# A transformer-like block in fp32r halves: one 64-column stationary for both mLSTM gates, and the last batch's steps in another order

## The chip, the cores and the metric

The kernel runs on one core of one Trainium2 chip. The metric is the device time of one execution in microseconds; several runs are taken and their median is quoted. A profiled execution gives a span, from its first to its last instruction, and a trace of every engine: PE is TensorE, DVE is VectorE, ACT is ScalarE, POOL is GpSimd, SP is SyncE, whose queue issues the DMAs here.

## What is computed

Four layers on 4 batches of 256 tokens, width 256: attention, a gated FFN, an mLSTM block with its own MLP, and an int8 FFN, with a layer norm after each. The change touches the mLSTM block, which in the reference is

```python
h_in = _rmsnorm(x, norm1_w)
q = (h_in @ wq).reshape(B, S, H, dqk).transpose(0, 2, 1, 3)      # k, v alike
o_pre = h_in @ w_og
i_pre = _soft_cap(h_in @ w_ig + b_ig).transpose(0, 2, 1)         # 8 heads, cap * tanh(x / cap)
f_pre = _soft_cap(h_in @ w_fg + b_fg).transpose(0, 2, 1)
h = _mlstm_parallel(q, k, v, i_pre, f_pre)
...
logfg = jax.nn.log_sigmoid(f_pre)
Fcum = jnp.cumsum(logfg, axis=-1)
Dmat = Fcum[..., :, None] - Fcum[..., None, :] + i_pre[..., None, :]     # causal
m = jnp.max(Dmat, axis=-1, keepdims=True)
C = qk * jnp.exp(Dmat - m)
n = jnp.maximum(jnp.abs(jnp.sum(C, axis=-1, keepdims=True)), jnp.exp(-m))
h = jnp.einsum('bhst,bhtd->bhsd', C / n, v)
```

## The kernel before

Every fp32 product is made of three: each operand is held as a high part and a remainder (`xTh`, `xTl`; `WLh`, `WLl`), and PE adds high by high, high by remainder and remainder by high. So `six` issues 6 matmuls for a contraction over 256, and the activations of a batch stand transposed in `xh_v[:, :, c, :]` and `xl_v[:, :, c, :]`, 256 columns for a batch `c`.

Every engine's program is written out by hand in one order, and each engine runs its own in order; semaphores tie them. The stretch that the change touches lies between the end of the first FFN (`ffn_pe(pe, 0)`) and the mLSTM heads:

- **The last batch.** Batches 0 to 2 have been normed and transposed inside the first FFN. Batch 3 comes behind it: `add_out(dve, 0, 3)`, `dve_stats`, `pool_ln`, `dve_apply` (layer norm), `act_ssq`, `pool_rms`, `dve_xs` (rms norm into `xs`), `pe_T(pe, 1, 3)` (4 transposes into the PSUM bank `TB`), `act_hi` and `dve_lo` (the two parts of `xT`, which raise `xt_split`).
- **The projections on PE.** For each batch `project_qk` (2 x 12 matmuls of 256 columns into `UG[0]` and `UG[1]`) and `project_vog` (2 x 6 of 512 columns into `UG[2]` and `UG[3]`). ACT and DVE empty the banks: `evac_q`, `evac_k`, `evac_og` on ACT, `split_q`, `split_k`, `take_v` on DVE. The next batch may write a bank when `qk_split` or `og_ready` says so.
- **The gates.** `project_gates(c)` makes the rows of the input gate and of the forget gate, 8 heads each. A window of a padded weight (`WIDE` = 96 + 128 columns) puts batch `c`'s heads into rows 32c to 32c + 7 of a 128-row sum; both gates and all four batches are added up into two banks, `X[:, 0:S]` and `OUTS[:, 1, 0:S]`: 12 matmuls of 256 columns per batch. When all four are in, ACT's `gates` takes both banks (2 Tanh of 128 x 256), then Exp and Ln, which needs another function table, and loads the table of Tanh again for `evac_og(1)`.
- **The rows.** DVE's `chain` (two scans, two adds) makes the running sums `cumS`, `gr`, their maxima `M` and `nm`. SP writes `M` to DRAM (`scr_m`) and reads it back broadcast over 128 partitions, batch 0 in four quarters (`m_first`), batches 1 to 3 in two halves each (`m_rows`) into the buffer `A[c % 2]`; `m_rows(c, half)` for c > 1 waits on `e_ready`, that is for the decays of batch c - 2 of the same heads. PE's `rows_T` transposes `gr` and `nm`.
- **The MLP's weights.** 12 pieces of 128 x 512 come through a ring of 5 buffers `raw`. ACT takes the high part (`mlp_hi`), POOL the remainder (`split_mlp`), SP loads the next (`more`).
- **The heads.** `heads(c)` runs through 4 pairs of heads. PE: `scores` (L1521, L1522) of the next pair, `values` (L1536 to L1540), `back` of the pair before (L1549), and in between `heads_T` (L1561), `project_out`, `pe_T` of an earlier batch, and a filler `keep_busy` (L1578). ACT: `take_pair`, then `decay` of the two heads that come 4 heads later (L1693, L1694). DVE: `weigh` of two heads (L1880), `mask_rows` (L1871: adds the causal mask to two heads' rows in `A`), and for an earlier batch `norm_b` (L1907, L1912), `hoT`, `head_sums`, `add_heads`. POOL's `head_scales` (L2056) makes the scales that `norm_b` needs, and PE's `heads_T` waits for `norm_b`.

## Time and profile before

| | |
|---|---|
| median of 3 runs | 673.22 us (672.23 to 675.36) |
| the profiled execution | 672.34 us, of which the span is 670.6 us |
| PE busy | 658.1 us, 98% of the span |
| DVE, ACT, POOL busy | 438.3, 411.3, 246.7 us |
| granted TensorE clock, mean | 0.995 |
| last matmuls of the first FFN | 473.42 us |
| projections and gates on PE | 473.76 to 502.92 us |
| heads | 502.92 to 540.70 us |

Times in the trace are microseconds from the start of the span. A matmul's record is longer than the step to the next one, because the array is pipelined and its end is modelled: a 256-column matmul shows 0.28 us, and the next one starts 0.12 us later. What a matmul costs in a full stream is therefore read from start to start.

### The profile page before, as it was taken

How to read it: one execution, taken by the hardware profiler on the slowest of the kernel's cores; microseconds unless marked ns; L12 is line 12 of the kernel's file. 1: busy time of each engine (PE TensorE's matmuls, PEld its weight loads, DVE VectorE, ACT ScalarE, POOL GpSimd, SP SyncE). 2: the span in 40 equal slices, each digit the busy share in tenths (PEclk: the TensorE clock that was granted, in tenths of full speed). 3: DMA queues.
4: the chain of work that ended last, by engine and by line, in shares of the span. 5: the costliest groups of instructions: out<-in, count | busy, mean ns of one | idle time of the engine just before them, and what ended most of it. 6: DMA issues, size and time to landing. Idle time of an engine off the chain costs nothing. (4 is left out here: it accounts for less than half of the span.)

```text
span 670.6 us, 15275 instructions
## 1 busy us (share of the span) xinstructions
PE 658.1 (98%) x5297; PEld 633.0 (94%) x5297; DVE 438.3 (65%) x968; ACT 411.3 (61%) x1085; POOL 246.7 (37%) x279
## 2 busy tenths in 40 slices
PE   8999999999999999999999999999999999999995
PEld 8999999999999999999999899999987799999995
DVE  6556557557666655765665576556569986556877
ACT  5556677666776666866577773334689864333553
POOL 3731972134353133632328555112451462222011
PEclk9999999999999999999999999999999899999999
DMA  7174654435534436534363404000166100000000
GB/s 254 37 219 160 193 172 140 133 101 174 168 127 113 127 108 185 161 128 126 97 183 124 111 1 151 32 0 2 48 208 243 65 1 1 1 1 0 1 33 31
DMA packets 38172, 69.74 MB, mean 104 GB/s; under 512 B 3440, under 2 KB 22640, under 8 KB 37872
## 3 DMA queue, kind: packets, MB, share of 16 engines
q1 hardware_dynamic: 37696, 68.38, 32.8%
q10 hardware_dynamic: 432, 0.79, 0.4%
q8 instruction: 26, 0.43, 0.3%
q14 instruction: 18, 0.15, 0.1%
HBM read 52.18 MB, written 16.97 MB: 103 GB/s over the span
## 5 line engine op out<-in xcount | busy, mean ns | idle before, releaser
L312 PE MATMUL PJ<-xTh,WBh 128*128 128x256 f32 x364 | 106.7, 293 | 0.3 <-POOL WBl L839 0.3
L314 PE MATMUL PJ<-xTh,WBl 128*128 128x256 f32 x364 | 103.0, 283 | 0.0
L313 PE MATMUL PJ<-xTl,WBh 128*128 128x256 f32 x364 | 102.8, 283 | 0.0
L824 POOL TENSOR_TENSOR stage<-stage 128x256 f32<-128x256 f32 x32 | 24.5, 766 | 165.0 <-DVE stage L691 165.0
L584 ACT ACTIVATE probs<-probs,rinv 128x256 f32<-128x256 f32 x128 | 58.4, 507 | 26.7 <-DVE rinv L707 26.7
L1202 PE MATMUL UG<-xTh,WBh 128*128 (+1 forms) x256 | 73.6, 288 | 0.3 <-PEq L54 0.3
L1205 PE MATMUL UG<-xTh,WBl 128*128 (+1 forms) x256 | 72.4, 283 | 0.0
L1203 PE MATMUL UG<-xTl,WBh 128*128 (+1 forms) x256 | 72.4, 283 | 0.0
L1274 ACT ACTIVATE ga<-UG 128x256 f32<-128x256 f32 x64 | 24.5, 383 | 75.1 <-PE UG L1205 75.1
L312 PEld LDWEIGHTS PJ<-xTh,WBh 128*128 128x128 f32 x364 | 69.6, 191 | 0.9 <-issue 0.5
L313 PEld LDWEIGHTS PJ<-xTl,WBh 128*128 128x128 f32 x364 | 69.6, 191 | 0.0
L314 PEld LDWEIGHTS PJ<-xTh,WBl 128*128 128x128 f32 x364 | 69.4, 191 | 0.0
L696 DVE TENSOR_TENSOR QKl<-PJ,QKh 128x512 fp32r<-128x512 f32 x63 | 43.4, 689 | 36.5 <-ACT QKh L572 36.3
L1326 DVE TENSOR_TENSOR gb<-UG,ga 128x256 f32<-128x256 f32 x64 | 27.1, 423 | 44.4 <-ACT ga L1274 43.8
L1061 POOL TENSOR_SCALAR vare<-mv 128x2 f32<-128x2 f32 x13 | 2.9, 224 | 131.9 <-DVE mv L1054 131.9
L839 POOL TENSOR_TENSOR WBl<-raw,WBh 128x512 fp32r<-128x512 f32 x32 | 40.8, 1295 | 28.4 <-ACT WBh L601 28.4
L577 ACT ACTIVATE probs<-TB,nmax 128x256 f32<-128x256 f32 x64 | 29.8, 470 | 33.7 <-DVE nmax L703 32.2
L577 ACT ACTIVATE probs<-SC,nmax 128x256 f32<-128x256 f32 x64 | 29.8, 471 | 32.6 <-DVE nmax L703 32.5
L1202 PEld LDWEIGHTS UG<-xTh,WBh 128*128 128x128 f32 x256 | 49.0, 192 | 0.5 <-issue 0.5
L1203 PEld LDWEIGHTS UG<-xTl,WBh 128*128 128x128 f32 x256 | 49.0, 192 | 0.0
L1205 PEld LDWEIGHTS UG<-xTh,WBl 128*128 128x128 f32 x256 | 49.0, 191 | 0.0
L701 DVE TENSOR_REDUCE rmax<-TB 128x2 f32<-128x512 f32 x32 | 22.1, 692 | 39.8 <-PE TB L393 35.4
(320 smaller groups left out, 2385.9 us busy)
## 6 DMA issues: line engine op xcount, KB each, us to landing
K<-scr_k SPq DMA_DIRECT2D x60, 256.0 KB, 4.3
raw<-in_w_att SPq DMA_DIRECT2D x37, 256.0 KB, 4.7
Q<-scr_q SPq DMA_DIRECT2D x15, 512.0 KB, 7.5
stage<-scr_m SPq DMA_DIRECT2D x6, 768.0 KB, 5.9
scr_q<-rot_h SPq DMA_DIRECT2D x30, 128.0 KB
scr_q<-rot_l SPq DMA_DIRECT2D x30, 128.0 KB
scr_k<-rot_h SPq DMA_DIRECT2D x30, 128.0 KB
scr_k<-rot_l SPq DMA_DIRECT2D x30, 128.0 KB
```

The lines of the kernel that those rows point to most:

```text
L312: pe.matmul(out, ah, bh, start=(i == 0), stop=False)
L313: pe.matmul(out, ah, bl, start=False, stop=False)
L314: last = pe.matmul(out, al, bh, start=False, stop=(i == n - 1))
L577: last = act.activation(probs[:, j % 2, t, :], SC[j % 2][:, t, :], ACT.Exp, scale=SCALE, bias=nmax[:, j % 2, t:t + 1], accum_out=rsum[:, j ...
L584: last = act.activation(probs[:, j % 2, t, :], probs[:, j % 2, t, :], ACT.Copy, scale=rinv[:, j % 2, t:t + 1])
L696: dve.tensor_tensor(part_dst(k, p, False), bank_of(k, p)[:, :], part_dst(k, p, True).bitcast(F32), ALU.subtract).then_inc(part_split, 1)
L824: pool.tensor_tensor(y[:, 0:S], c[:, 0:S], sn[:, S:2 * S], ALU.subtract).then_inc(rope_sum, 1)
L839: pool.tensor_tensor(weights(i, False), raw[:, i % RING, :], weights(i, True).bitcast(F32), ALU.subtract).then_inc(w_split, 1)
L1202: pe.matmul(out, wh, xh_v[:, t, c, :], start=(t == 0), stop=False)
L1203: last = pe.matmul(out, wh, xl_v[:, t, c, :], start=False, stop=(kind == 2 and t == KT - 1))
L1205: last = pe.matmul(out, w_up(kind, t, ht, which, False), xh_v[:, t, c, :], start=False, stop=(t == KT - 1))
L1326: dve.tensor_tensor(y, u, ga[:, ht % 2, 0:S], ALU.mult).then_inc(q["gated"], 1)
```

## The change

Both gates' weights are packed without padding into one stationary of 64 columns (32 for the input gate, 32 for the forget gate; 8 of each are used). One stream through it gives both gates of a batch in 64 rows. `project_gates(0, 2)` takes batches 0 and 1 in one stream of 512 columns, `project_gates(2)` and `project_gates(3)` take 256 each: 6 matmuls a call, 18 in all instead of 48. Each batch has its own region (`gate_sums[c]`: the halves of `X` for batches 0 and 1, the halves of `OUTS[:, 1]` for 2 and 3). ACT's `gates_tanh(c)` copies a batch's 2 x 32 rows through Tanh into rows 32c of `gt`, 8 activations instead of 2. Before `project_gates(3)` writes into the bank of batch 2's sums, PE waits for the Tanh of batch 2.

The rest is order. PE: the gates of batches 0 to 2 stand between the first three parts of the projections, batch 3's in the middle of batch 1's k. ACT: two conversions of MLP pieces move behind batch 0's q and k, the Tanh of batches 0 to 2 stand right behind `act_ssq`, `act_hi(1, 3)` goes ahead of `evac_og(0)`, Exp and Ln stand around `evac_k(1)`, and the conversions of pieces 10 and 11 go into the first two pairs of heads. DVE: `split_q(0)` and `split_k(0)` stand within the last batch's norm. SP: pieces 10 and 11 are loaded behind batch 0's quarters of the rows and ahead of the other batches'. In batch 2's first pair, DVE adds the mask to batch 3's first two quarters ahead of `norm_b(0)`; before, one of them stood behind it and the other one in the next pair.

On PE, where the first projection of batch 0 ended and its v and og parts stood, the kernel before has (`UG<-WLh,xTl` is the end of `project_vog(0)`):

```order
L1457 MATMUL UG<-WLh,xTl 128x512
L1474 MATMUL X<-xTh,WI 128x256
L1474 MATMUL X<-xTl,WI 128x256
L1474 MATMUL X<-xTh,WI 128x256 x2
L1474 MATMUL X<-xTl,WI 128x256
L1474 MATMUL X<-xTh,WI 128x256
L1474 MATMUL OUTS<-xTh,WI 128x256
```

and the changed one (`UG<-xTh,WLl` is the end of batch 0's k, `UG<-WLh,xTh` the start of its v and og):

```order
L1458 MATMUL UG<-xTh,WLl 128x256
L1475 MATMUL X<-xTh,WI 64x512
L1475 MATMUL X<-xTl,WI 64x512
L1475 MATMUL X<-xTh,WI 64x512 x2
L1475 MATMUL X<-xTl,WI 64x512
L1475 MATMUL X<-xTh,WI 64x512
L1456 MATMUL UG<-WLh,xTh 128x512
```

The two sums of 128 rows became one of 64 rows, over two batches at once, and stand ahead of v and og.

On ACT, from the gates to batch 1's og, the kernel before has (`WBh<-raw` is `mlp_hi`, `gt` the gates, `x<-UG` is `evac_og`):

```order
L1736 ACTIVATE WBh<-raw 128x512
L1673 ACTIVATE gt<-X,bgs 128x256
L1673 ACTIVATE gt<-OUTS,bgs 128x256
L1678 ACTIVATE gt<-gt 128x256
L1680 ACT_TABLE_LOAD
L1680 ACTIVATE gt<-gt 128x256
L1667 ACT_TABLE_LOAD
L1667 ACTIVATE x<-UG 128x256 x2
```

and the changed one (`WI<-UG,cols` is `evac_k(1)`):

```order
L1750 ACTIVATE WBh<-raw 128x512
L1684 ACTIVATE gt<-OUTS,bgs 32x256 x2
L1690 ACTIVATE gt<-gt 128x256
L1668 ACTIVATE WI<-UG,cols 128x512
L1694 ACT_TABLE_LOAD
L1694 ACTIVATE gt<-gt 128x256
L1750 ACTIVATE WBh<-raw 128x512
L1675 ACT_TABLE_LOAD
L1675 ACTIVATE x<-UG 128x256 x2
```

Both table loads stay, and between the gates' Exp and Ln stands batch 1's k.

On DVE, in batch 2's first pair, the kernel before has (`stage<-stage,mask` is `mask_rows`, `ho` is `norm_b`):

```order
L1880 SCALAR_TENSOR_TENSOR gb<-UG,ga 128x384 x2
L1907 TENSOR_TENSOR ho<-hraw,hsc 128x256 x2
L1912 SCALAR_TENSOR_TENSOR ho<-x,ho 128x512
L1871 TENSOR_TENSOR stage<-stage,mask 128x2x2x128
L1880 SCALAR_TENSOR_TENSOR rows<-UG,rows 128x384 x2
```

and the changed one:

```order
L1901 SCALAR_TENSOR_TENSOR gb<-UG,ga 128x384 x2
L1892 TENSOR_TENSOR stage<-stage,mask 128x2x2x128 x2
L1928 TENSOR_TENSOR ho<-hraw,hsc 128x256 x2
L1933 SCALAR_TENSOR_TENSOR ho<-x,ho 128x512
L1901 SCALAR_TENSOR_TENSOR rows<-UG,rows 128x384 x2
```

The norm moved behind both masks.

```diff
...
-        gate_w = WI[:, :, :].rearrange("p a n -> p (a n)")[:, 12 * PIECE - 4 * KT * WIDE:]
-        WGh, WGl = (gate_w[:, i * 2 * KT * WIDE:(i + 1) * 2 * KT * WIDE].rearrange("p (t g n) -> p t g n", t=KT, g=2)
-                    for i in range(2))
+        gate_w = WI[:, 11, PIECE - 4 * KT * 32:].rearrange("p (l t n) -> p l t n", l=2, t=KT)
+        WGh, WGl = gate_w[:, 0], gate_w[:, 1]
+        WG_parts = [gate_w[:, l].rearrange("p t (g n) -> p t g n", g=2) for l in range(2)]
...
-        wg_f = stage1[:, 0:2 * KT * WIDE].rearrange("p (t g n) -> p t g n", t=KT, g=2)
+        wg_f = stage1[:, 0:2 * KT * WIDE].rearrange("p (t g n) -> p t g n", t=KT, g=2)[:, :, :, 96:128]
...
-        gate_sums = (X[:, 0:S], OUTS[:, 1, 0:S])
+        gate_sums = [bank[0:2 * 32, i * S:(i + 1) * S] for bank in (X[:, :], OUTS[:, 1, :]) for i in range(2)]
...
-            more(RING, 12)
+            more(RING, 10)
             sp.wait_ge(s_["m_ready"], 1)
             out_rows = scr_m.rearrange("c h n -> (c h) n")
             sp.dma_start(out_rows[:, 0:S], M[:, :]).then_inc(s_["m_out"], 16)
...
             sp.wait_ge(s_["m_out"], 32)
             for quarter in range(4):
                 m_first(quarter)
+            more(10, 12)
             for c in range(1, B):
                 for half in range(2):
                     m_rows(c, half)
...
             def x_parts(c):
                 return [(xh_v[:, t, c, :], xl_v[:, t, c, :]) for t in range(KT)]
-            def project_gates(c):
-
-                pe.wait_ge(s_["xt_split"], N_T[1] + c + 1)
+            def project_gates(c, n=1):
+
+                pe.wait_ge(s_["xt_split"], N_T[1] + c + n)
                 if c == 0:
                     pe.wait_ge(s_["wg_split"], 1)
                     pe.wait_ge(s_["x_added"], N_ADD[3])
-
-                w = slice(96 - 32 * c, 96 - 32 * c + P)
-                for n, out in enumerate(gate_sums):
-                    for i in range(3 * KT):
-                        t, (a, b) = i // 3, ((WGh, xh_v), (WGh, xl_v), (WGl, xh_v))[i % 3]
-                        last = pe.matmul(out, a[:, t, n, w], b[:, t, c, :], start=(c == 0 and i == 0),
-                                         stop=(c == B - 1 and i == 3 * KT - 1))
+                if c == B - 1:
+                    pe.wait_ge(s_["gates_tanh"], B - 1)
+                out = X[0:2 * 32, :] if n == 2 else gate_sums[c]
+                for t in range(KT):
+                    for i, (w, x) in enumerate(((WGh, xh_v), (WGh, xl_v), (WGl, xh_v))):
+                        last = pe.matmul(out, w[:, t, :], x[:, t, c:c + n, :], start=(t == 0 and i == 0),
+                                         stop=(t == KT - 1 and i == 2))
                 last.then_inc(s_["gates_ready"], 1)
-            def project_qk(c):
+            def project_part(c, i, which=range(2)):
                 if c == 0:
                     pe.wait_ge(s_["wl_split"], LP - 1)
-                for i in range(2):
-                    if c:
-                        pe.wait_ge(s_["qk_split"], 2 * c - 1 + i)
-                    for n in range(2):
-                        w = slice((2 * i + n) * P, (2 * i + n + 1) * P)
-                        last = six(UG[i][:, n * S:(n + 1) * S], [(WLh[:, t, w], WLl[:, t, w]) for t in range(KT)],
-                                   x_parts(c))
+                else:
+                    pe.wait_ge(s_["qk_split"], 2 * c - 1 + i)
+                for n in which:
+                    w = slice((2 * i + n) * P, (2 * i + n + 1) * P)
+                    last = six(UG[i][:, n * S:(n + 1) * S], [(WLh[:, t, w], WLl[:, t, w]) for t in range(KT)],
+                               x_parts(c))
+                if which[-1] == 1:
                     last.then_inc(s_["qk_ready"], 1)
...
             def project(c):
-                project_qk(c)
-                project_vog(c)
+                project_part(c, 0)
+                project_part(c, 1)
+                project_vog(c, 0)
+                project_vog(c, 1)
             def rows_T():
...
                     if pair == 1 and c >= 3:
                         pe_T(pe, 2, c - 3)
-            project(0)
-            for c in range(B - 2):
-                project_gates(c)
+            project_part(0, 0)
+            project_part(0, 1)
+            project_gates(0, 2)
+            project_vog(0, 0)
+            project_gates(2)
+            project_vog(0, 1)
             pe_T(pe, 1, B - 1)
-            project_gates(B - 2)
-            project_qk(1)
-            project_gates(B - 1)
-            project_vog(1)
+            project_part(1, 0)
+            project_part(1, 1, range(1))
+            project_gates(3)
+            project_part(1, 1, range(1, 2))
+            project_vog(1, 0)
+            project_vog(1, 1)
             project(2)
             rows_T()
             project(3)
...
         def _(act):
             ffn_act(act, 0)
             act.wait_ge(s_["wg_in"], 16)
-            act.activation(WGh, wg_f, ACT.Copy).then_inc(s_["wg_hi"], 1)
+            act.activation(WG_parts[0], wg_f, ACT.Copy).then_inc(s_["wg_hi"], 1)
             act.wait_ge(s_["small_in"], 16 * 4)
             act.activation(nn[:, 0:1], cols[:, C_LO:C_LO + 1], ACT.Exp)
...
                     act.wait_ge(s_["v_taken"], 2 * c + t + 1)
                     act.activation(og_v[:, c, t, :], UG[2 + t][:, D:2 * D], ACT.Tanh, scale=0.5).then_inc(s_["og_ready"], 1)
-            def gates():
-                act.wait_ge(s_["gates_ready"], B)
-                act.wait_ge(s_["bgs_ready"], 1)
+            def gates_tanh(c):
+
+                act.wait_ge(s_["gates_ready"], max(c, 1))
+                if c == 0:
+                    act.wait_ge(s_["bgs_ready"], 1)
                 for n in range(2):
-                    last = act.activation(gt[:, n, :], gate_sums[n], ACT.Tanh, scale=1.0 / CAP,
-                                          bias=bgs[:, n:n + 1])
+                    at = slice(32 * n, 32 * n + 32)
+                    last = act.activation(gt[32 * c:32 * c + 32, n, :], gate_sums[c][at, :], ACT.Tanh, scale=1.0 / CAP,
+                                          bias=bgs[at, n:n + 1])
                 last.then_inc(s_["gates_tanh"], 1)
-                act.wait_ge(s_["gates_tanh"], 1)
+            def gates_exp():
+                act.wait_ge(s_["gates_tanh"], B)
                 act.activation(gt[:, 1, :], gt[:, 1, :], ACT.Exp, scale=-CAP).then_inc(s_["gates_tanh"], 1)
-                act.wait_ge(s_["gates_tanh"], 2)
+
+            def gates_log():
+                act.wait_ge(s_["gates_tanh"], B + 1)
                 act.activation(gt[:, 1, :], gt[:, 1, :], ACT.Ln, bias=1.0).then_inc(s_["sp_ready"], 1)
             def exp_nm():
...
                         act.wait_ge(ffn_sems[0]["down"], FT * B)
                     act.activation(mlp_place(i, True), raw[:, i % RING, :], ACT.Copy).then_inc(s_["wm_hi"], 1)
-            mlp_hi(0, 5)
+            mlp_hi(0, 2)
+            evac_q(0)
+            mlp_hi(2, 3)
+            evac_k(0)
+            mlp_hi(3, 4)
             act_ssq(act, 1, 3)
-            evac_q(0)
-            evac_k(0)
+            for c in range(3):
+                gates_tanh(c)
+            act_hi(act, 1, 3)
             evac_og(0)
-            act_hi(act, 1, 3)
+            evac_q(1)
+            mlp_hi(4, 5)
+            gates_tanh(3)
+            gates_exp()
+            evac_k(1)
+            gates_log()
             mlp_hi(5, 6)
-            evac_q(1)
+            evac_og(1)
+            evac_q(2)
             mlp_hi(6, 7)
-            evac_k(1)
-            mlp_hi(7, 8)
-            gates()
-            evac_og(1)
-            mlp_hi(8, 9)
-            evac_q(2)
+            evac_k(2)
+            mlp_hi(7, 9)
+            evac_og(2)
             mlp_hi(9, 10)
-            evac_k(2)
-            mlp_hi(10, 12)
-            evac_og(2)
             exp_nm()
             evac_q(3)
             evac_k(3)
...
                     for u in (HM * c + 2 * pair + 4, HM * c + 2 * pair + 5):
                         if u < HM * B:
                             decay(u // HM, u % HM)
+                    if c == 0 and pair < 2:
+                        mlp_hi(10 + pair, 11 + pair)
                     if pair == 2 and c >= 3:
                         act_hi(act, 2, c - 3)
                     if pair == 3 and c >= 2:
...
             dve_stats(dve, 0, B - 2)
             ffn_dve(dve, 0)
             dve.wait_ge(s_["wg_hi"], 1)
-            dve.tensor_tensor(WGl, wg_f, WGh.bitcast(F32), ALU.subtract).then_inc(s_["wg_split"], 1)
+            dve.tensor_tensor(WG_parts[1], wg_f, WG_parts[0].bitcast(F32), ALU.subtract).then_inc(s_["wg_split"], 1)
             dve.wait_ge(s_["small_in"], 64)
             dve.tensor_scalar(bgs[:, :], bg[:, :], 1.0 / CAP, None, ALU.mult).then_inc(s_["bgs_ready"], 1)
...
             add_out(dve, 0, 3)
             dve_stats(dve, 1, 3)
+            split_q(0)
             dve_apply(dve, 1, 3)
+            split_k(0)
             dve_xs(dve, 1, 3)
-            split(0)
+            take_v(0, 0)
+            take_v(0, 1)
             dve_lo(dve, 1, 3)
             split(1)
             chain()
...
                     if c == 0 and pair == 0:
                         mask_rows(0, 2)
                         mask_rows(0, 3)
+                    if (c, pair) == (2, 0):
+                        mask_rows(3, 0)
+                        mask_rows(3, 1)
                     if pair == 0 and c >= 2:
                         norm_b(c - 2)
                     if pair == 1 and c >= 3:
...
                     if c == 0 and pair == 3:
                         mask_rows(1, 2)
                         mask_rows(1, 3)
-                    if c in (1, 2):
-                        mask_rows(c + 1, pair)
+                    if c == 1:
+                        mask_rows(2, pair)
+                    if c == 2 and pair >= 2:
+                        mask_rows(3, pair)
             def finish_heads(k, c, ht):
                 if ht == 0:
```

## Rows read from the trace of the kernel before

**Rows 1.** The page: the span, and the granted clock in 40 slices.
```profile
span 670.6 us, 15275 instructions
PEclk9999999999999999999999999999999899999999
```

**Rows 2.** Stretches: us; busy PE, PEld, DVE, ACT, POOL; clock; DMA share; GB/s.
```profile
503.00:512.00 9.00, 8.79 (x98) 6.78 (x98) 8.46 (x17) 8.57 (x26) 0.00 (x0) 1.00 0.76 297
520.00:524.00 4.00, 4.00 (x29) 2.70 (x27) 3.47 (x7) 2.96 (x9) 0.46 (x1) 0.62 0.61 241
531.00:540.00 9.00, 8.88 (x97) 7.05 (x96) 8.93 (x20) 7.52 (x24) 5.22 (x8) 1.00 0.01 4
560.00:600.00 40.00, 40.00 (x337) 40.00 (x337) 24.12 (x60) 14.81 (x43) 9.48 (x15) 1.00 0.01 2
```

**Rows 3.** Timeline of PE, projections and gates: start, duration, line, operation.
```profile
473.76 0.28 PE L1455 MATMUL UG<-xTh,WLh 128*128 128x256 f32 x1
...
476.63 0.40 PE L1455 MATMUL UG<-WLh,xTh 128*128 128x512 f32 x1
...
479.38 0.29 PE L1474 MATMUL X<-xTh,WI 128*128 128x256 f32 x1
...
482.25 0.60 PE L1119 MATMUL TB<-ident,xs 128*128 128x128 f32 x4
...
486.98 0.28 PE L1474 MATMUL X<-xTh,WI 128*128 128x256 f32 x1
...
488.42 0.40 PE L1455 MATMUL UG<-WLh,xTh 128*128 128x512 f32 x1
...
494.03 0.40 PE L1455 MATMUL UG<-WLh,xTh 128*128 128x512 f32 x1
...
502.92 0.39 PE L1521 MATMUL UG<-WI 32*128 32x256 f32 x2
```

**Rows 4.** Timeline of PE in the heads: stationaries of 33 columns.
```profile
509.40 0.39 PE L1538 MATMUL UG<-gb,V 128*33 128x128 f32 x4
509.62 0.39 PE L1540 MATMUL UG<-gb,V 128*33 128x128 f32 x4
```

**Rows 5.** Timeline of ACT: MLP pieces, the gates' tables, the heads.
```profile
474.57 2.70 ACT L1736 ACTIVATE WBh<-raw 128x512 fp32r<-128x512 f32 x5
...
489.92 1.28 ACT L1680 ACT_TABLE_LOAD   x1
491.22 0.42 ACT L1680 ACTIVATE gt<-gt 128x256 f32<-128x256 f32 x1
...
492.95 0.66 ACT L1667 ACTIVATE x<-UG 128x256 f32<-128x256 f32 x2
...
511.45 0.39 ACT L1694 ACTIVATE rows<-stage,gcol 128x128 f32<-128x128 f32 x1
...
513.98 0.38 ACT L1702 ACTIVATE gt<-UG 97x256 f32<-97x256 f32 x1 [0.37 <-PE UG L1540]
...
522.78 0.38 ACT L1702 ACTIVATE gt<-UG 97x256 f32<-97x256 f32 x1 [0.82 <-PE UG L1540]
```

**Rows 6.** Timeline of DVE: batch 3's norm and split, the chain, batch 2's first pairs.
```profile
480.38 0.62 DVE L1102 TENSOR_SCALAR xs<-xres,rrms 128x256 f32<-128x256 f32 x2 [2.16 <-POOL rrms L1096]
...
484.16 0.87 DVE L1143 SCALAR_TENSOR_TENSOR xTl<-TB,cols,xTh 128x256 fp32r<-128x256 f32 x2 [1.18 <-ACT xTh L1131]
...
491.70 0.68 DVE L1833 TENSOR_TENSOR_SCAN rows<-rows,gt 128x256 f32<-128x256 f32 x1
...
520.50 0.76 DVE L1907 TENSOR_TENSOR ho<-hraw,hsc 128x256 f32<-128x256 f32 x2 [0.65 <-POOL hsc L2056]
...
521.90 0.69 DVE L1871 TENSOR_TENSOR stage<-stage,mask 128x512 f32<-128x512 f32 x1
...
524.86 1.02 DVE L1880 SCALAR_TENSOR_TENSOR gb<-UG,ga 128x384 f32<-128x384 f32 x2 [0.74 <-PE UG L1522]
```

**Rows 7.** The line of `m_rows` (L1419), 6 transfers: from issue to landing.
```profile
DMA to landing us min/median/max: 4.1/5.9/9.0
```

13 lines of the change are left out of this document (6 added, 7 removed).

## Prediction

> **What bounds the kernel now.** I read the page first, then stretches, then the timelines of the engines around the gates, then the heads. The page gives a span of 670.6 us with TensorE granted full clock in all but one slice [rows 1]. The stretches split the span into two kinds. In the MLP behind the heads (560 to 600 us) PE is busy for all 40.00 us while DVE has 24 and ACT 15 [rows 2]: whatever time PE gets earlier is passed on unchanged to the end. In the heads it is close between three engines: from 503 to 512 us DVE has 8.46, ACT 8.57 and PE 8.79 of 9 us, and from 531 to 540 DVE has 8.93 of 9 [rows 2]. Between them, from 520 to 524, the granted clock is 0.62: TensorE ran part of it at 1.2 instead of 2.4 GHz [rows 2]. The reader should see in the timeline of PE that the projections and gates form one full stream from 473.76 to 502.92 us: 24 matmuls of 256 columns take 476.63 - 473.76 = 2.87 us (0.1196 each), 12 of 512 take 479.38 - 476.63 = 2.75 us (0.229 each), and the 24 of the gates of batches 0 and 1 take 482.25 - 479.38 = 2.87 us [rows 3]. So in this stretch PE's instructions are the bound, and each one removed is worth its step, until another engine is late.
>
> **Gates: 48 matmuls become 18.** Removed: 48 x 0.1196 = 5.74 us; the last 12 of them read 488.42 - 486.98 = 1.44 us [rows 3], the same rate. Added: 6 of 512 columns, 6 x 0.229 = 1.37, and 12 of 256, 12 x 0.1196 = 1.44, together 2.81. Net **-2.93 us** on PE. No row has a 64-column stationary. A 33-column one in the heads streams 4 x 128 columns in 509.62 - 509.40 = 0.22 us, 0.055 each [rows 4], which is half of the 256-column step with 128 columns of weights; so a narrower stationary costs neither more nor less per streamed column, and I take the rate as it is. The nearest rows on both sides, 33 and 128 columns, agree, so the range of this term is narrow; half the rate is a rival below.
>
> **Waits that the denser stream can run into.** With 2.93 us less PE work, the engines that feed PE must be earlier as well.
> - Transposes of batch 3 (`pe_T`). PE came to them at 482.25; now it has 1.37 + 0.72 of gates ahead instead of 2.87, so 481.47. `xs` was done at 480.38 + 0.62 = 481.00 [rows 6]. It may come 0.4 earlier, since the gate weights' conversions shrink from 896 to 128 columns; the two splits put between the norm's steps fill holes (DVE idled 2.16 us ahead of `xs` [rows 6]). No wait, 0.5 us to spare.
> - Gates of batch 3. PE is there at 481.47 + 0.4 + 18 x 0.1196 = 484.05. Their input needs the transposes (0.60), `act_hi` and `dve_lo` (about 0.87 each by the row at 484.16): 481.47 + 0.60 + 0.87 + 0.87 = 483.8. The other end is the distance of before, 485.03 - 482.25 = 2.78, which gives 484.25 [rows 3, 6]. Wait: 0 to 0.2. The new wait for the Tanh of batch 2 ends sooner: its sums are in at 480.3, and two activations of 256 columns take 0.66 (the row at 492.95) [rows 5]. Behind this PE wait all later projections are queued, so what it costs is passed on.
> - og of batch 1 before v and og of batch 2. PE gets there at 494.03 - 2.93 = 491.10 [rows 3]. On ACT the last gates are in at 484.05 + 0.72 + 0.2 = 484.97; Tanh, Exp and batch 1's k take about 0.8 + 0.4 + 0.6, so the first table load starts near 486.8. Before, og started 492.95 - 489.92 = 3.03 us behind that load, with Ln and the second load in it; an MLP piece comes in between, 2.70 / 5 = 0.54 [rows 5]. og starts at 490.35, its first half is done at 490.75, 0.35 before PE wants it. Wait: 0, at most 0.3.
> - Rows. The chain began at 491.70 [rows 6]; Ln now ends near 488.5 and batch 1's last v is taken at 488.8, so it begins 2.9 us sooner, with PE's shift. Nothing gains beyond that, because no mask of batch 0 waited for its rows.
>
> A table switch shows 491.22 - 489.92 = 1.30 us from the load to the next activation [rows 5]. The Trainium skill, "ScalarE: Activation LUTs", section "What ACT_TABLE_LOAD costs", counts a load and a drain, about 2.66 us for every switch; with its 1.36 more for each of the two switches og would come 2.7 us later, PE would wait 2.35, and the time would be 672.4. The row contradicts it for these very tables; I leave it 1 chance in 100.
>
> **Pieces 10 and 11 on ACT within the heads.** 2 x 0.54 = 1.08 us more where ACT has 8.57 of 9 us [rows 2, 5]. `take_pair` and the decays behind them move back. ACT then waits for PE by 0.37 us at 513.98 and by 0.82 at 522.78 [rows 5], together 1.19: the delay is gone by then, and the decays are made four heads ahead of their use. Cost 0, at most 1.08 - 0.37 = 0.7. Their loads (2 x 256 KB) stand ahead of batch 1's rows in SP's queue; at the 297 GB/s of [rows 2] that is 1.7 us, and batch 1's first mask comes over 10 us behind its issue, against 9.0 for the longest transfer [rows 7]. Cost 0.
>
> **The two masks.** DVE waited 0.65 us for POOL ahead of `norm_b(0)` at 520.50 [rows 6]. Two masks (0.68 us recorded, 0.6 each in a row) now fill it and push the norm by 0.6 us: its end goes from 521.90 to 522.5. The next `weigh` began behind norm and mask at 522.5 and still does. The mask that stood behind it is gone, but DVE waits there for PE's scores (0.74 us at 524.86 [rows 6]), so that wait only grows. PE's `heads_T` needs the norm; at the low clock PE reached it only about 523. Value: 0 while the norm ends before 523. No DMA is issued by the moved steps; the rows of batch 3 that the masks read are weighed below.
>
> **Sum.** 672.34 - 2.93 = 669.4 for an execution like the profiled one, which lies 0.88 below the median of the runs; 673.22 - 2.93 = 670.3 by the median. With some tenth for the tight waits I forecast **670.0 us**, between the two.
>
> **Rivals.**
> - *The low clock goes away (chance 0.18).* The fall comes in a stretch where PE has short gaps, and everything there moves 2.9 us earlier with another pattern of waits. Against it: the pattern is nearly that of before. At full clock DVE's 0.74 us wait for the scores goes; behind it DVE is full, so all of it is passed on: 670.0 - 0.7 = 669.3. The other way, a fall twice as long, costs about as much, 670.7. The Trainium skill, "TensorE: Matmul & The Clock Gate", section "What's actually happening", says that the window in which activity is judged runs free of the kernel, so that the same work can be cut another way; no run here shows it yet, and it is why I give this rival more than nothing.
> - *New waits eat part of it (0.22).* 0.2 at the gates of batch 3, 0.3 at og, 0.7 from ACT in the heads, the longest of each: 670.0 + 1.2 = 671.2. For it: the first two have slack of only 0.2 to 0.35 us.
> - *The cost is not in the columns (0.05).* If a 512-column stream through 64 columns ran at half the rate, the gates would cost 5.6 us and nothing would be won: 672.9. The 33-column rows speak against it.
> - *Slower (0.04): DVE waits for batch 3's rows.* Their DMA is released when the decay ending at 511.45 + 0.39 = 511.84 is done [rows 5], with the ACT delay up to 512.9. The first moved mask wants them at 519.85 in the old clock. A landing after 5.9 us (median) comes in time at 518.8, one after 9.0 at 521.9 [rows 7]: 2.0 us in which norm, `weigh` and with them PE stand still. A gap like that would lengthen the low clock as well, by another 1.52 us for each stretch like 520 to 524 (4.00 x 0.38) [rows 2]. Together 3.5, more than the 2.93 won: 670.0 + 3.5 = 673.5. It decides from a landing about 521.3 on.
>
> **How the numbers follow.** The forecast, 669.4 to 670.7 as its own range, has 0.50; the clock 0.18, new waits 0.22, the columns 0.05, the slower rival 0.04, the table 0.01. The range for 8 in 10 reaches from a bit below the clock's case to above the new waits with the spread of the runs before (1 us below the median): **668.5 to 672.0**. About 0.5%, 3.37 us, is what a measurement of this kernel can tell from no change; that is 669.85. Below it lies 0.24 of the forecast's 0.50, since 670.0 stands just above it, and of the clock's case 0.12, together faster 0.36. Slower by as much, over 676.6, would need the slower rival's transfer to land another 3 us later: 0.02 of its 0.04. Within: 0.62.
>
> **What would show it.** Right: 18 matmuls at 0.229 and 0.12 steps on the gates' line, and `scores(0, 0)` starting at about 500.0 instead of 502.92; the FFNs unchanged in length. PE's list of waits shows nothing at the gates of batch 3 nor at batch 2's v and og. ACT's waits at 513.98 and 522.78 shrink by 1.1 together. DVE's 0.65 us wait for POOL is gone, and that for the scores is longer. Wrong: scores later than 500.5, a wait of DVE for a DMA of `stage` in batch 2, or another stretch with a low clock.

## The result, and the profile after

The changed kernel takes 681.88 us (median of 4 runs, 681.8 to 682.1), the kernel before 672.91 (4 runs beside them). The ratio is 1.0127, interval 1.0101 to 1.0153: **9.0 us slower**, where 670.0 was forecast and 672.0 was the top of the range. The profiled execution took 681.83 us. The executions of several kernels below spread over some 10 us together with their mean granted clock, and there the times are given with that clock.

The page of after, as [rows 1]:

```profile
span 680.0 us, 15222 instructions
PEclk9999999999999999999999999999995699999998
```

The clock row holds the outline of the answer: two slices at 5 and 6 tenths, where before one slice had 8. The stretches, with the columns of [rows 2], are first two long ones and then single microseconds around the fall and the return:

```profile
503.00:512.00 9.00, 7.65 (x68) 5.91 (x65) 6.47 (x12) 7.35 (x21) 2.56 (x2) 0.76 0.76 317
520.00:534.00 14.00, 14.00 (x96) 9.68 (x95) 9.05 (x21) 8.91 (x26) 3.65 (x4) 0.50 0.31 114
...
506.00:507.00 1.00, 0.00 (x0) 0.00 (x0) 1.00 (x3) 1.00 (x4) 0.11 (x2) 1.00 0.98 412
507.00:508.00 1.00, 0.89 (x6) 0.89 (x7) 1.00 (x3) 0.95 (x4) 1.00 (x1) 0.84 0.95 393
508.00:509.00 1.00, 1.00 (x10) 0.83 (x10) 1.00 (x2) 0.64 (x2) 0.19 (x1) 0.50 1.06 442
...
537.00:538.00 1.00, 1.00 (x8) 0.75 (x9) 0.17 (x1) 0.00 (x0) 0.62 (x1) 0.50 0.00 0
538.00:539.00 1.00, 1.00 (x14) 0.75 (x10) 1.00 (x2) 0.04 (x1) 0.00 (x0) 0.80 0.00 0
```

From about 507.7 to 538.4 us, 30.7 us long, TensorE was granted 1.2 GHz. It showed itself 14.00 of 14 us busy there, while DVE had 9.05 and ACT 8.91: at the low clock PE is the bound of the heads, which it isn't at the full one. Before, the clock was low for 3.4 us, from about 520.9 to 524.3, of which [rows 2] show the part up to 524; two rows of before:

```profile
521.00:524.00 3.00, 3.00 (x19) 1.97 (x18) 2.97 (x6) 1.96 (x5) 0.00 (x0) 0.50 0.51 210
524.00:525.00 1.00, 1.00 (x10) 0.87 (x9) 0.26 (x2) 0.88 (x3) 0.00 (x0) 0.83 0.00 0
```

Ahead of the fall of after there is one microsecond in which PE did nothing.

PE's timeline of after, from the gates to the fall and to the end of the low clock, answers to [rows 3]:

```profile
476.89 0.39 PE L1475 MATMUL X<-xTh,WI 128*64 128x512 f32 x1
...
478.27 0.39 PE L1456 MATMUL UG<-WLh,xTh 128*128 128x512 f32 x1
...
479.64 0.28 PE L1475 MATMUL OUTS<-xTh,WI 128*64 128x256 f32 x1
...
480.33 0.40 PE L1456 MATMUL UG<-WLh,xTh 128*128 128x512 f32 x1
...
481.72 0.60 PE L1119 MATMUL TB<-ident,xs 128*128 128x128 f32 x4
...
484.30 0.28 PE L1475 MATMUL OUTS<-xTh,WI 128*64 128x256 f32 x1
...
491.32 0.47 PE L1456 MATMUL UG<-WLh,xTh 128*128 128x512 f32 x1
...
500.29 0.39 PE L1524 MATMUL UG<-WI 32*128 32x256 f32 x2
...
507.11 0.38 PE L1524 MATMUL UG<-WI 32*128 32x256 f32 x1 [1.13 <-DVE gb L1901]
...
510.50 0.59 PE L1524 MATMUL UG<-WI 32*128 32x256 f32 x2
...
513.50 0.59 PE L1524 MATMUL UG<-WI 32*128 32x256 f32 x2
...
534.87 0.58 PE L1456 MATMUL X<-WLh 128*128 128x256 f32 x1
```

The gates came as forecast: six matmuls of 512 columns through the 64-column stationary in 478.27 - 476.89 = 1.38 us, six of 256 in 0.69. `scores(0, 0)` starts at 500.29 instead of 502.92, 2.63 us sooner. The last matmul of L1202, in the last FFN, starts at 670.5 instead of 661.0, 9.5 later. Between the two, each place against its place before: `scores(0, 6)` 508.54 to 507.11, so 1.43 sooner and 1.2 already lost; the first matmul of `project_out(0)` 526.90 to 534.87, now 7.97 later, 9.40 lost on the way; behind it another 1.5, of which 12 matmuls that step by 0.213 instead of 0.12 make 1.1. So **about 1.2 us went into the wait and 10.9 into the stretch behind it**, where PE never stood still and most of the time had the low clock. The step from one pair of heads to the next is 513.50 - 510.50 = 3.00 us; before, six pairs went from 508.54 to 520.07, 1.92 each.

What made the gap stands in the other engines' timelines. DVE of after (start, duration, line, operation, [idle before it, and for what]):

```profile
489.79 1.42 DVE L1856 SCALAR_TENSOR_TENSOR rows<-gt,rows 128x256 f32<-128x256 f32 x1
...
505.89 0.69 DVE L1892 TENSOR_TENSOR stage<-stage,mask 128x512 f32<-128x512 f32 x1 [1.74 <-DMA stage<-scr_m]
506.50 1.02 DVE L1901 SCALAR_TENSOR_TENSOR gb<-UG,ga 128x384 f32<-128x384 f32 x2
507.44 1.30 DVE L1892 TENSOR_TENSOR stage<-stage,mask 128x512 f32<-128x512 f32 x1
```

POOL and SP's queue of after:

```profile
489.62 1.30 POOL L2090 TENSOR_TENSOR WBl<-raw,WBh 128x512 fp32r<-128x512 f32 x1 [2.37 <-ACT WBh L1750]
...
506.91 1.28 POOL L2090 TENSOR_TENSOR QKl<-raw,QKh 128x512 fp32r<-128x512 f32 x1 [0.89 <-ACT QKh L1750]
```

```profile
493.98 2.71 SPq L1412 DMA_DIRECT2D stage<-scr_m  x4
496.79 0.85 SPq L1425 DMA_DIRECT2D raw<-in_wm_d  x2
497.69 0.90 SPq L1419 DMA_DIRECT2D stage<-scr_m  x2
```

And three rows of before, not shown so far: the same issue of batch 1's rows on SP, the chain's second step and batch 1's first mask on DVE:

```profile
497.42 1.64 SPq L1419 DMA_DIRECT2D stage<-scr_m  x2
```

```profile
492.41 0.43 DVE L1835 SCALAR_TENSOR_TENSOR rows<-gt,rows 128x256 f32<-128x256 f32 x1
...
506.70 0.68 DVE L1871 TENSOR_TENSOR stage<-stage,mask 128x512 f32<-128x512 f32 x1
```

The heads start 2.63 us sooner, and the rows of batch 1 that they need are issued 0.27 *later* (497.42 to 497.69). The chain does start 2.64 sooner (489.06 instead of 491.70); it loses 0.99 in its second step, 0.97 in the issues of `m_first` (2.71 instead of 1.74) and 0.94 in the two loads of pieces now ahead. The mask wants the rows at 504.15, they land at 505.87.

The trace of before has the slack that was used up: there the same transfer took 7.69 us and landed at 505.10, 1.60 ahead of the mask at 506.70. The two loads alone would have left 0.7 of it. With them, the chain's step, the issues of `m_first` and a transfer of 8.18 us instead of 7.69, it is 1.60 - 0.94 - 0.99 - 0.97 - 0.49 = -1.8, and DVE waited 1.74.

### The profile page after: what moved, and what is told of

Same layout as the page of the kernel before. It is cut to its first block and busy times, and to the rows that moved or that the text cites. A ratio compares the mean times of both kernels' runs of the same rounds, so it can differ in the third digit from the quotient of the medians.

```text
span 680.0 us, 15222 instructions
## 1 busy us (share of the span) xinstructions
PE 666.6 (98%) x5267; PEld 637.1 (94%) x5267; DVE 440.9 (65%) x968; ACT 413.6 (61%) x1091; POOL 246.6 (36%) x279
## 5 line engine op out<-in xcount | busy, mean ns | idle before, releaser
L1202 PE MATMUL UG<-xTh,WBh 128*128 (+1 forms) x256 | 73.6, 288 | 0.3 <-PEq L54 0.3
L1202 PEld LDWEIGHTS UG<-xTh,WBh 128*128 128x128 f32 x256 | 49.0, 192 | 0.5 <-issue 0.5
```

The costliest lines, as they stand in the source:

```text
L1202: pe.matmul(out, wh, xh_v[:, t, c, :], start=(t == 0), stop=False)
```

## The experiments

Each is an edit of the changed kernel unless it says that it starts from before. They asked three things: which wait made the gap, whether the gap made the low clock, and whether the rest of the change works without it.

**The rows of batch 1 ahead of the two loads.**

```diff
-            more(10, 12)
-            for c in range(1, B):
+            m_rows(1, 0)
+            m_rows(1, 1)
+            more(10, 12)
+            for c in range(2, B):
```

> The changed kernel with one thing undone in part: SP issues batch 1's two transfers of rows ahead of the loads of pieces 10 and 11, not behind them. Theory A (late rows break the clock): in the changed kernel DVE waited 1.74 us for batch 1's rows, PE then 1.13 us for DVE, and right there the granted clock fell to 1.2 GHz for some 25 us. Here the rows are issued 0.9 us sooner and 512 KB less stand ahead of them, 1.6 us at 325 GB/s, together more than the 1.74 us wait: no wait, no long low clock, 670 to 671 us. Theory B (the added ACT work of pieces 10 and 11 in the heads starves DVE and PE): no change, 681 to 682 us. Theory C (the 64-column gates or the denser order itself lowers the clock): no change, 681 to 682 us.

681.57 us, ratio 1.0124 (1.0092 to 1.0156). The wait for batch 1's rows was gone, and the time stayed. ACT and PE of this kernel:

```profile
508.13 0.63 ACT L1752 ACTIVATE QKh<-raw 128x512 fp32r<-128x512 f32 x1 [2.48 <-DMA raw<-in_wm_d]
```

```profile
509.08 0.39 PE L1554 MATMUL OUTS<-ident,gt 97*128 97x97 f32 x2 [1.92 <-ACT gt L1718]
```

Now the load of piece 10 is late, ACT waits for it in the first pair of heads, and PE behind ACT. Another gap, the same low clock. My expectation was wrong: two transfers share one short time, and putting one first only chose which is late.

**The two pieces back ahead of the heads**, in loading and in conversion.

```diff
-            more(RING, 10)
+            more(RING, 12)
...
-            more(10, 12)
...
-            mlp_hi(9, 10)
+            mlp_hi(9, 12)
...
-                    if c == 0 and pair < 2:
-                        mlp_hi(10 + pair, 11 + pair)
```

> The changed kernel with pieces 10 and 11 as before: loaded ahead of the rows, converted by ACT ahead of the heads. Theory A: the two loads no longer stand between batch 0's and batch 1's rows, so the rows come in time and the time is 670 to 671 us. Theory B: the ACT work is out of the heads, also 670 to 671 us; against the run with the rows first this tells A from B. Theory C: 681 to 682 us.

686.27 us, 1.0195 (1.0168 to 1.0223), worse. Again my expectation was missed. With ACT's new order the earlier pieces are converted late, so the two loads hold SP's queue until 496.08, ahead of `scr_m`; DVE's first mask of batch 0, which stands ahead of batch 3's k, waits 1.77 us for its rows, and PE waits for the heads' first operands:

```profile
505.11 0.39 PE L1523 MATMUL UG<-WI 32*128 32x256 f32 x2 [2.96 <-DVE WI L1867]
```

With the rest of the order as changed, the two pieces can't simply stay ahead of the heads.

**The masks back behind the norm**, as before.

```diff
-                    if (c, pair) == (2, 0):
-                        mask_rows(3, 0)
-                        mask_rows(3, 1)
...
-                    if c == 1:
-                        mask_rows(2, pair)
-                    if c == 2 and pair >= 2:
-                        mask_rows(3, pair)
+                    if c in (1, 2):
+                        mask_rows(c + 1, pair)
```

> The changed kernel with the norm ahead of both masks of batch 3 again, as before. Theory A: the fall comes 15 us ahead of this place, so the long low clock stays and the time is within 1 us of 681.9. Theory D (the two masks wait for batch 3's rows and hold the norm back): 670 to 672 us.

683.15 us, 1.0142 (1.0121 to 1.0164); PE's gap is 1.11 us at the same place. The moved masks are not the cause.

**The gap filled.** Five filler matmuls of 512 columns where PE stood still, and nothing else.

```diff
                         keep_busy(1)
+                    if (c, pair) == (0, 1):
+                        keep_busy(5)
```

> The changed kernel with 5 filler matmuls of 512 columns (1.15 us of PE) ahead of the values of batch 0's second pair, where PE later waits 1.13 us. DVE's wait for the rows stays. Theory A, with the gap on PE as what lets the clock fall: PE is busy through the wait, the clock stays at 2.4 GHz, and only the stall of about 1 us is left: 671 to 672 us. If the clock falls for another reason than this gap: 681 to 683 us.

**672.13 us**, 0.9991 (0.9964 to 1.0019): 9.75 us less for 5 matmuls that compute nothing. DVE still waited, and the fillers stand in PE's gap:

```profile
506.91 1.24 DVE L1894 TENSOR_TENSOR stage<-stage,mask 128x512 f32<-128x512 f32 x1 [1.20 <-DMA stage<-scr_m]
```

```profile
506.37 1.43 PE L1581 MATMUL TB<-WLh 128*128 128x512 f32 x5
```

From 503 to 520 us the clock is 0.99 to 1.00. In the profiled execution (674.9 us, the longest of the four) it then falls where before had its fall, behind a gap of 0.29 us, and is low for 6.8 us, to 526.7:

```profile
520.00:534.00 14.00, 14.00 (x124) 10.39 (x125) 10.96 (x24) 10.62 (x32) 5.38 (x5) 0.76 0.25 93
```

This run separates the two: the late rows by themselves cost little; that PE stood still at this place cost about 10 us.

**Both transfers given time**: rows first, and the two conversions in pairs 2 and 3 instead of 0 and 1. In the second kernel the conversion whose subtraction stood beside the chain moves as well.

```diff
-                    if c == 0 and pair < 2:
-                        mlp_hi(10 + pair, 11 + pair)
+                    if c == 0 and pair >= 2:
+                        mlp_hi(8 + pair, 9 + pair)
```

> The changed kernel with batch 1's rows issued ahead of pieces 10 and 11, and with their conversions on ACT in the third and fourth pair of batch 0 instead of the first two. In the run with the rows first alone, ACT waited 2.48 us for piece 10, which landed at 508.1; in the third pair ACT comes to it about 509. Theory A2 (any gap of over 1 us on PE between 505 and 509 us lets the clock fall, and it then stays at 1.2 GHz until batch 0's output projection; which transfer is late is indifferent): no gap is left, the clock is near 0.99, 670 to 672 us. Theory C (the 64-column gates or the denser order lowers the clock by itself): 680 us or more.

```diff
             gates_log()
-            mlp_hi(5, 6)
             evac_og(1)
             evac_q(2)
+            mlp_hi(5, 6)
```

> The same, and on ACT piece 5's conversion stands behind batch 1's og and batch 2's q instead of ahead of them, so that POOL's subtraction for it does not run beside DVE's chain. In the changed kernel the chain's second step took 1.42 us beside POOL, against 0.43 before, and M was 1 us late. Expected: that step at 0.43 us, rows about 1 us sooner, no gap in the heads, 669.5 to 671.5 us. If the 1.42 us is not POOL's doing it stays.

678.23 us, 1.0085 (1.0047 to 1.0123), and 679.32 us, 1.0085 (1.0052 to 1.0117). I had expected 672 us or less. No transfer is waited for in the heads of either. Rows of the first (DVE, PE), then the chain's step in the second:

```profile
507.03 2.36 DVE L1894 TENSOR_TENSOR stage<-stage,mask 128x512 f32<-128x512 f32 x2
```

```profile
509.91 0.38 PE L1526 MATMUL UG<-WI 32*128 32x256 f32 x1 [0.97 <-DVE gb L1903]
```

```profile
491.26 0.43 DVE L1858 SCALAR_TENSOR_TENSOR rows<-gt,rows 128x256 f32<-128x256 f32 x1
```

The step is back at 0.43 once no subtraction runs beside it. And there is a second cause of a gap: two masks take 2.36 us instead of 1.28 because POOL's subtractions of pieces 10 and 11, which follow ACT's conversions into the heads, run beside them.

**The kernel before with the new gates alone**: 64-column stationary, 18 matmuls, the 8 Tanh in one place, no other order.

```diff
-            for c in range(B - 2):
-                project_gates(c)
+            project_gates(0, 2)
             pe_T(pe, 1, B - 1)
...
+                for c in range(B):
+                    for n in range(2):
+                        at = slice(32 * n, 32 * n + 32)
+                        last = act.activation(gt[32 * c:32 * c + 32, n, :], gate_sums[c][at, :], ACT.Tanh,
+                                              scale=1.0 / CAP, bias=bgs[at, n:n + 1])
```

> The kernel before with the 64-column gates alone: batches 0 and 1 in one stream, the calls where they were, the 8 Tanh all together when the last gates are in, everything else as before. Theory A2: PE's stream is 2.9 us shorter, but the 8 Tanh cost ACT some 2.4 us more ahead of Exp, so the rows come at about the old time while the heads start up to 2.9 us sooner; if they then wait over 1 us, PE gets a gap and the low clock: 675 to 685 us. If the rows are just in time: 670 to 671. Theory C (narrow gates lower the clock in the projections themselves): the granted clock falls ahead of 500 us, which no run so far shows.

677.21 us, 1.0070 (1.0047 to 1.0093). PE and ACT of this kernel:

```profile
496.33 0.79 PE L1455 MATMUL UG<-WLh,xTh 128*128 128x512 f32 x1 [4.45 <-ACT x L1664]
```

```profile
488.61 1.89 ACT L1672 ACTIVATE gt<-X,bgs 32x256 f32<-32x256 f32 x4
490.51 1.90 ACT L1672 ACTIVATE gt<-OUTS,bgs 32x256 f32<-32x256 f32 x4
```

The Tanh became 3.8 us on ACT, og of batch 1 stands behind them, and PE waits 4.45 us for it, more than the matmuls saved. So the new order is not decoration: with the Tanh all in one place the gates are worth nothing. The clock fell behind this gap too, but it came back within the projections, where the matmuls stand close and PE is again the bound (stretches of 5 us, clock in the third column from the right):

```profile
495.00:500.00 5.00, 3.67 (x9) 2.90 (x10) 3.67 (x7) 4.88 (x10) 2.85 (x3) 0.50 0.19 63
500.00:505.00 5.00, 5.00 (x34) 4.51 (x33) 1.53 (x4) 1.55 (x4) 2.16 (x2) 0.84 0.96 307
505.00:510.00 5.00, 5.00 (x33) 3.70 (x32) 4.30 (x9) 4.12 (x11) 0.00 (x0) 1.00 0.73 301
```

From about 501.6 us on it is full, up to a fall of 3.4 us at 525.5, which answers to the one of before. So the narrower stationary itself does not bring the low clock, and the longest gap of all was followed by less low clock in the projections (6.8 us, the first 1.6 of them still within the gap) than gaps of 0.39 to 1.92 us in the heads (23.9 us and more).

**The kernel before with the two pieces late**: loads behind `m_first`, conversions in the first two pairs.

```diff
-            more(RING, 12)
+            more(RING, 10)
...
+            more(10, 12)
...
-            mlp_hi(10, 12)
...
+                    if c == 0 and pair < 2:
+                        mlp_hi(10 + pair, 11 + pair)
```

> The kernel before with the change's part on pieces 10 and 11 alone: loaded between batch 0's and batch 1's rows, converted by ACT in the first two pairs of heads. Gates and all else as before. Batch 1's rows are then issued about 0.9 us later and 512 KB stand ahead of them, but here the heads start 2.7 us later than in the changed kernel, so DVE's first mask of batch 1 is asked for at 508.2. Theory A2: the rows are there in time or up to 1 us late, no long low clock, 672 to 674 us. If it is the order of the transfers by itself that costs the 9 us: 680 to 683 us.

676.93 us, 1.0080 (1.0043 to 1.0117), and split: three of 8 executions at a clock of 0.993 or more take 673.66 to 675.0 us, two at 0.988 take 676.9 and 677.0, three at 0.979 to 0.981 take 679.8 to 683.2; 672 to 674 was expected. In the profiled one, of the first kind, PE's gap was 0.40 us. The rows were in time there; ACT waited 1.0 us for piece 10, and the masks beside POOL's subtractions took up to 1.79 us for two.

**The kernel before with POOL's work beside the masks alone**: two subtractions that nobody uses, released by the decays.

```diff
+            for done in (8, 10):
+                pool.wait_ge(s_["wm_split"], done // 2 + 8)
+                pool.wait_ge(s_["e_ready"], done)
+                pool.tensor_tensor(raw[:, 4, :], raw[:, 3, :], raw[:, 3, :], ALU.subtract).then_inc(s_["wm_split"], 1)
```

> The kernel before plus two POOL subtractions of 128 x 512 from SBUF to SBUF, whose result nobody reads, at the places where batch 0's third and fourth pair run. No transfer, no ACT work and no PE work is added or moved. Theory E: masks beside them take 1.0 to 1.3 us instead of 0.68, PE gets a gap of 0.3 to 1 us near 513, and the time goes up, run by run differently, to between 673 and 683 us. If only ACT's work or the transfers matter: 672 to 673 us, as before.

678.90 us, 1.0069 (1.0039 to 1.0098, without the longest execution); two of 10 executions at a clock of 0.998 take 673.0 us, three at 0.988 take 676.6 to 677.1, five at 0.977 to 0.985 take 680.7 to 683.3. Nothing else of the change is in this kernel. DVE, POOL and PE of the profiled one (681.77 us):

```profile
510.78 2.13 DVE L1871 TENSOR_TENSOR stage<-stage,mask 128x512 f32<-128x512 f32 x2
```

```profile
509.17 1.24 POOL L2071 TENSOR_TENSOR raw<-raw 128x512 f32<-128x512 f32 x1 [9.32 <-ACT rows L1694]
510.86 1.50 POOL L2071 TENSOR_TENSOR raw<-raw 128x512 f32<-128x512 f32 x1 [0.46 <-ACT ga L1694]
```

```profile
513.43 0.38 PE L1521 MATMUL UG<-WI 32*128 32x256 f32 x1 [0.75 <-DVE gb L1880]
```

**All causes taken away**: rows first, chain free, and both conversions with their subtractions late, behind `add_heads(0)` on POOL. First with the conversions in batch 3 (masks as changed, then as before), then in batch 2. So that the later subtractions can't hold PE up, it asks for the last MLP pieces only ahead of the MLP's first down product; this belongs to all four kernels that follow.

```diff
-                    if c == 0 and pair < 2:
+                    if c == 3 and pair < 2:
                         mlp_hi(10 + pair, 11 + pair)
...
-            split_mlp(0, 12)
+            split_mlp(0, 10)
...
             add_heads(0)
+            split_mlp(10, 12)
```

> The changed kernel with batch 1's rows ahead of pieces 10 and 11, piece 5's conversion behind batch 2's q, and the conversions of pieces 10 and 11 on ACT in batch 3's first two pairs, their subtractions on POOL behind add_heads(0); PE asks for the last pieces at the MLP's first down product. No mask of DVE then runs beside a POOL subtraction and no transfer is late. Theory E (POOL's subtraction beside DVE's masks doubles a mask from 0.68 to about 1.3 us, the pair grows over 1.7 us, PE gets a gap and the clock falls): the masks take 0.68 us, no PE wait over 0.3 us before batch 2, mean clock 0.995, and the whole gain of the gates is there: 669 to 671 us. Theory C (the change of the gates itself lowers the clock): 676 us or more.

> The first kernel of this set with the norm ahead of batch 3's masks again. It measures that part of the change with the clock intact. The prediction put it at 0: the same as the first within 0.3 us. With the norm later by 0.6 us it could also be up to 0.6 faster.

```diff
-                    if c == 3 and pair < 2:
+                    if c == 2 and pair < 2:
                         mlp_hi(10 + pair, 11 + pair)
```

> The gates and the order of the changed kernel with the causes taken out: rows ahead of the loads of pieces 10 and 11, piece 5 behind batch 2's q, the norm ahead of batch 3's masks as before, ACT's conversions of pieces 10 and 11 in batch 2's first two pairs, where ACT waits for PE by 0.8 us each, and POOL's subtractions behind add_heads(0). With the conversions in batch 3 PE waited 0.9 us for DVE's xs there, because ACT was late. Expected: no PE wait over 0.3 us between 480 and 540, heads 2.9 us earlier after the start of the first FFN, 670 to 671 us, 0.2 to 0.4% below the kernel before. If the gain of the gates is lost in the heads whatever the order is: 672 to 673 us.

With batch 3: 672.65 us, 0.9999 (0.9987 to 1.0011), where 669 to 671 was expected; PE waits 0.89 us in batch 3 for `xs`, because ACT is late there. With the masks back 671.33, 0.9981 (0.9966 to 0.9995). With batch 2 and the masks back: **670.82 us**, 12 runs from 669.88 to 673.91, ratio **0.9974 (0.9961 to 0.9987)**, the fastest of all. Its page, DVE and PE:

```profile
PEclk9999999999999999999999999999999999999998
```

```profile
507.33 1.28 DVE L1895 TENSOR_TENSOR stage<-stage,mask 128x512 f32<-128x512 f32 x2
```

```profile
532.86 0.66 PE L1119 MATMUL TB<-ident,xs 128*128 128x128 f32 x4 [0.55 <-DVE xs L1102]
```

Two masks take 1.28 us again, PE's longest gap in the heads is 0.55 us, near the end of them, and no slice of the heads has a low clock. From the first L1202 matmul to the last it has 401.7 to 658.5, 256.8 us; before, 401.6 to 661.0, 259.4: 2.6 us less. This is not the gates' gain alone. Up to `scores(0, 0)` (500.07, before 502.92) it is 2.9 us less, and from there to the last L1202 matmul 0.4 more, although the 3.4 us of low clock of before are missing, which at the price found below (0.36 us for each) is an estimated 1.2. So waits in the heads took some 1.6 us, and the full clock gave 1.2 back. Whether the masks behind the norm are better by the 1.3 us between the first two medians stays open: from first to last L1202 their profiled executions show 257.8 us with the masks as changed and 258.9 with them back, the other way round, but the second had 3.4 us of low clock from 518.7 us on and the first none. That start lies 401.3 to 403.5 us into the span in the profiled executions, which is ahead of everything changed and more than such a difference.

**The late rows alone**: conversions and subtractions as in the fastest kernel, but SP's order and the chain as changed, so that of the two causes only the late rows are left. (The masks of batch 3 are as changed too; undoing them alone, above, took nothing off.)

```diff
-                    if c == 0 and pair < 2:
+                    if c == 2 and pair < 2:
                         mlp_hi(10 + pair, 11 + pair)
```

> The changed kernel with only the POOL subtractions of pieces 10 and 11 taken away from DVE's masks (ACT converts them in batch 2's first two pairs, POOL subtracts behind add_heads(0)). The loads still stand ahead of batch 1's rows and the chain still runs beside POOL, so DVE's wait of 1.7 us for batch 1's rows stays. Theory A (the late rows are enough by themselves): PE gap of 1 us near 507, long low clock, 679 to 683 us. Theory E (only the slow masks do it): clock 0.99, 671 to 673 us.

Six of 10 executions take 670.2 to 672.25 us at a clock of 0.994 to 0.997, four take 680.82 to 683.86 at 0.971 to 0.978. The ratio 0.9972 (0.9958 to 0.9985) is that of the six. DVE and PE of a profiled execution of the second kind:

```profile
507.06 0.69 DVE L1893 TENSOR_TENSOR stage<-stage,mask 128x512 f32<-128x512 f32 x1 [1.00 <-DMA stage<-scr_m]
```

```profile
508.27 0.38 PE L1525 MATMUL UG<-WI 32*128 32x256 f32 x1 [0.39 <-DVE gb L1902]
```

The longest gap ahead of the fall (at about 509.6) was 0.39 us in that execution; one of 0.21 lay 2.5 us ahead of it. The 0.40 us of the kernel before with late pieces was not followed by a fall, in the one profiled, nor were 0.38 and 0.55 in the fastest kernel. So either cause alone, POOL's work or the late rows, tips the clock in some executions (at least 5 of 10, and 4 of 10); with both, all four executions of the changed kernel had it.

## Why the prediction was wrong

**Right: the gates.** Removed 5.74, added 2.81 was the sum; measured from the first L1202 matmul (401.57 and 401.82) to `scores(0, 0)` it is 101.35 us before and 98.47 after, 2.88 less, against 2.93. The steps are 0.23 and 0.115 us. `pe_T` came at 481.72 (481.47 forecast), gates of batch 3 at 484.30 (484.05; the terms add up to 484.02), without a wait, and 0.25 of either difference is that start; PE came to og at 491.32 (491.10), where the first step, 0.31 instead of 0.23 to the next matmul, hides a delay of 0.1. The table switches took the 1.30 us of [rows 5] (487.31 to 488.61, 489.56 to 490.86), which also closes the rival with the page's price for a switch. Scores at "about 500.0" came at 500.29. So the term of the gates holds. That it is passed on unchanged does not hold through the heads, not even in the fastest kernel, where waits there took some 1.6 us of it and a fuller clock gave 1.2 back.

**Wrong step 1, the rows.** The prediction said that "it begins 2.9 us sooner, with PE's shift", and that "batch 1's first mask comes over 10 us behind its issue, against 9.0 for the longest transfer. Cost 0." The first half came true: from the start of the first FFN the chain began 2.89 us sooner. The second did not. Over 10 us is right for batch 1's second mask, at 508.23; the first is at 506.70, 9.28 behind the issue. And that distance was taken from the trace of before without the edit's own effect on its two ends: the need moved 2.63 sooner with the heads, and the issue moved 0.27 later. 9.28 - 2.63 - 0.27 = 6.4 us is what was left, against a median of 5.9 and a longest of 9.0 in [rows 7]; the transfer took 505.87 - 497.69 = 8.2, and DVE waited 1.74. What could be had from the trace of before is less: with the two loads alone 8.3 us were left (9.28 - 0.94), so no wait by the 7.69 us that this transfer took there and 0.7 by the longest of all. The rest came from the chain's step beside POOL (0.99, the next point) and from `m_first` (0.97, open).

**Wrong step 2, POOL.** The two conversions were counted on ACT (1.08 us, hidden; with the gap filled PE's waits behind the fillers, up to 545 us, are 0.29 and 0.11 us, so nothing speaks against it) and their loads on SP. That each conversion releases a subtraction of 1.28 us on POOL, and that these move into the heads as well, stands in no line of the prediction. The order of POOL doesn't change, only its time, which is why the difference in order did not show it. There they stood beside DVE's masks, where DVE has 8.46 of 9 us [rows 2]. In the traces a mask that starts under a subtraction ends 0.55 us behind the subtraction's end. In the changed kernel 506.91 + 1.28 = 508.19 and 507.44 + 1.30 = 508.74; with POOL's work alone 510.86 + 1.50 = 512.36 and 510.78 + 2.13 = 512.91, where in turn the subtraction, before which a mask had begun, took 0.26 longer than the one at 509.17. `weigh`, one of whose inputs is in PSUM, keeps its 1.02 us beside them. The Trainium skill, "SBUF — State Buffer", section "Who interferes with whom", names this pair: a DVE instruction with two inputs in SBUF contends with a GpSimd one that reads SBUF, the lock is exclusive, and the order of issue decides which of the two is blocked. The rows of the subtractions agree in size and in both directions. Not every POOL instruction does it: beside POOL's power of 128 x 16 for the scales (520.34 in after, 2.92 us, both inputs in SBUF) the mask at 521.59 took its 0.68 us.

**Wrong step 3, the price of a gap.** The slower rival had the right shape: DVE waits for rows, PE behind it, the low clock grows. It named batch 3's rows, which were in time, and priced the clock at "another 1.52 us for each stretch like 520 to 524", 0.38 per us of low clock. The rate was about right, 10.9 us in 30.7 or 0.36 a microsecond; the length was not, 30.7 us for 4. In the heads PE has short matmuls with little between them, and at 1.2 GHz it shows itself full without the clock's return (14.00 of 14 us at 0.50, above). What ended the low stretch no run isolates: before, the clock was full again at about 524.3, within 1 us of the transposes of `heads_T(0)` (from 523.02); after, the same transposes at 529.09 did not end it, and it was over only at 538.4, 0.8 us behind the 12 matmuls of `project_out(0)`. With the new gates alone it lasted 6.8 us, in the projections. Over all profiled executions the length goes with the place of the fall and not with the gap: eight falls between 506.9 and 514.3 us lasted 23.9 to 37.6 us, and each ended 3.3 to 4.8 us behind the first matmul of `project_out(0)`; five falls from 518.7 us on, behind gaps of 0.28 to 0.30 us, lasted 3.4 or 6.8. By which rule no run here shows. The chance of "slower" was 0.04 for the rival and 0.02 beyond 0.5%: it was put on a transfer of batch 3 being late, when any wait of PE in the first 12 us of the heads could do it.

**What remains open.** Which of two like gaps tips the clock. One program gives 673.0 in one execution and 681 in another, so it isn't the program's order alone. The Trainium skill, "TensorE: Matmul & The Clock Gate", section "What's actually happening", says that the window in which activity is judged runs free of the kernel; the splits (6 and 4 of 10, 2 and 8 of 10) would fit that but do not show it, and the prediction quoted it only in the rival in which the low clock goes away. Also open is why one issue of `m_first` took 0.97 us longer; no run varied it.

## What to carry to other kernels

When an edit makes a stage shorter, work out both ends of every distance between a transfer's issue and its first use again, the use by its shift and the issue by its own and by what is now queued ahead of it; that a transfer was in time is a fact of the old schedule. When a step moves, follow it to the engine that it releases: POOL's subtractions moved into the heads without a line of POOL's program changing, and beside DVE work with both inputs in SBUF a subtraction of 1.28 us took up to 1.08 us from DVE. Where PE runs short matmuls nearly full, price a gap of half a microsecond as a possible low clock over the whole stretch, not as its own length; a few filler matmuls in the gap (here 5, worth 9.75 us) are the quick test of it.
